# A transformer layer on one core: the first tile gets its own program, and step 0 of the loop moves up in its queues

## The reference

```python
q, k, v = split(x @ w_qkv.T);  q, k = rope(q), rope(k)
scores = (q @ k.T) * 32 ** -0.5;  keep where 0 <= row - key < 64
x = layernorm(x + (softmax(scores) @ v) @ w_out.T)
gate = silu((x @ w_gate) * s_gate);  up = (x @ w_up) * s_up
x = layernorm(x + ((gate * up) @ w_down) * s_down)
```

## Time and profile before

| | us |
|---|---|
| median of 3 runs (lowest, highest) | 1300.38 (1298.34, 1301.97) |
| the profiled execution: its own time | 1294.35 |
| its span, first to last instruction | 1292.5 |
| PE, DVE, ACT, POOL busy | 1212.9, 970.7, 571.3, 377.1 |

### The profile page before, as it was taken

One profiled execution on the slowest core, in us unless ns is written; L12 is line 12 of the kernel. 1 busy time (PEld: TensorE's weight loads), 2 busy tenths in 40 slices (PEclk: granted clock), 3 DMA queues, 4 the chain that ended last, 5 costly groups with the idle time before them and its releaser, 6 DMA issues.

```text
span 1292.5 us, 24588 instructions
## 1 busy us (share of the span) xinstructions
PE 1212.9 (94%) x8200; PEld 548.4 (42%) x8200; DVE 970.7 (75%) x2797; ACT 571.3 (44%) x1608; POOL 377.1 (29%) x370
## 2 busy tenths in 40 slices
PE   8624999999999999999999999999999999999997
PEld 3212444444444444444444444444444444444443
DVE  6855799757997489965897669975799658996543
ACT  1464168502774038810586017840388205870230
POOL 1032115410353104521055102441045210551331
PEclk9855999999999999999999999999999999999999
DMA  9953484334654265441943337542655508443000
GB/s 328 231 109 68 98 151 95 78 64 91 123 95 90 51 114 99 99 86 41 160 101 60 78 80 134 98 87 42 117 107 96 95 34 158 100 65 71 33 1 33
DMA packets 345912, 124.74 MB, mean 97 GB/s; under 512 B 309056, under 2 KB 329792, under 8 KB 345792
## 3 DMA queue, kind: packets, MB, share of 16 engines
q1 hardware_dynamic: 337776, 108.32, 43.9%
q10 hardware_dynamic: 4896, 8.52, 1.8%
q0 software_dynamic: 3120, 6.29, 1.6%
HBM read 27.67 MB, written 8.39 MB: 28 GB/s over the span
## 4 chain that ended last, share of the span: by engine, by line
PE 40%; issue 28%; POOL 11%; DVE 9%; DMA 4%; ACT 4%; SPq 3%; POOLq 0%; DVEq 0%; ACTq 0%
PE bank L420 31%; PE bank L523 6%; POOL xT_sb L363 5%; POOL fuse L368 4%; DMA xT_sb<-xT_sb 2%; DVE fuse L705 2%; PE bank L491 2%; ACT probs L630 2%; DVE fuse L721 1%; SPq L282 1%; DMA qkT<-fuse 1%; DVE largest L833 1%; SPq L288 1%; PE bank L471 1%; POOL x L380 1%
## 5 line engine op out<-in xcount | busy, mean ns | idle before, releaser
L420 PE MATMUL bank<-wqkv,xT_sb 128*128 128x512 f32 x760 | 332.8, 598 | 1.1 <-DMA wqkv<-w_qkvT 0.8
L363 POOL TENSOR_TENSOR xT_sb<-probs,xT_sb 128x512 f16<-128x512 f32 x120 | 142.5, 1187 | 487.1 <-ACT xT_sb L588 487.1
L630 ACT ACTIVATE probs<-bank,neg_max,qk_scale 128x128 f32<-128x128 f32 x512 | 227.2, 455 | 71.1 <-DVE neg_max L761 51.1
L420 PE MATMUL bank<-x1T,wg 128*128 128x512 f16 (+1 forms) x1032 | 243.0, 378 | 0.9 <-DVE ffn_tmp L768 0.9
L420 PE MATMUL bank<-x1T,wu 128*128 128x512 f16 x1024 | 241.9, 379 | 0.0
L588 ACT ACTIVATE fuse<-fuse 128x512 f16<-128x512 f32 x128 | 70.0, 617 | 360.0 <-DVE fuse L711 351.9
L523 PE MATMUL bank<-wd,fuse 128*128 128x512 f16 x1024 | 222.3, 379 | 0.0
L420 PEld LDWEIGHTS bank<-wqkv,xT_sb 128*128 128x128 f32 x760 | 144.0, 191 | 181.4 <-issue 179.1
L368 POOL TENSOR_TENSOR fuse<-ffn_tmp,fuse 128x512 f16<-128x512 f32 x128 | 152.9, 1194 | 71.0 <-ACT fuse L588 69.2
L523 PEld LDWEIGHTS bank<-wd,fuse 128*128 128x128 f16 x1024 | 100.2, 98 | 123.1 <-issue 4.0
L420 PEld LDWEIGHTS bank<-x1T,wu 128*128 128x128 f16 x1024 | 100.2, 98 | 120.6
(11 more groups left out here) (95 smaller groups left out, 1018.8 us busy)
## 6 DMA issues: line engine op xcount, KB each, us to landing
xT_sb<-xT SPq DMA_DIRECT2D x36, 256.0 KB, 4.1
v_cross<-v_own SPq DMA_DIRECT2D x64, 128.0 KB, 2.6
qkT<-x SPq DMA_DIRECT2D x8, 1024.0 KB, 5.8
out<-y ACTq DMA_DIRECT2D x32, 256.0 KB, 2.3
wqkv<-w_qkvT SPq DMA_DIRECT2D x2, 1024.0 KB, 7.2
wd<-w_down POOLq DMA_DIRECT2D x1, 2048.0 KB, 10.7
wg<-w_gate POOLq DMA_DIRECT2D x1, 2048.0 KB, 14.3
wu<-w_up POOLq DMA_DIRECT2D x1, 2048.0 KB, 18.8
```

What stands on the lines that cost most here:

```text
L363: done(probs_low, pool.tensor_tensor(place[:, 1, :, :], probs[:, s % 2, :, :], place[:, 0, :, :], ALU.subtract))
L420: last = pe.matmul(dst, lhsT, rhs, start=(i == 0), stop=(i == len(pairs) - 1))
L630: last = act.activation(probs[:, s % 2, h, :], src, ACT.Exp, bias=neg_max[:, s % 2, h:h + 1], scale=qk_scale[:, 2:3], accum_out=row_sum[:, ...
```

## The change

Body(0) is replaced by a function of its own, `first`, on each engine; the body then serves the loop and the end alone.

In `first`, PE projects blocks 0 and 1 (even, odd, v of each), starts the scores of steps 0 and 1, and projects block 2 and block 3 between the steps; `project_o` of blocks 0, 1 and 2 stands behind steps 8, 12 and 15. The projections go round four banks (0 to 3). Rope of blocks 2 and 3 stands on DVE behind steps 1 and 5, `split_high` likewise on ACT. The low halves of blocks 1 to 3 are made by POOL, in the four subtractions that DVE made before; block 0 stays with DVE. The exponentials have four buffers instead of two; the two fp16 halves have two places instead of four; the transposed ones have four instead of two. The maximum of the next tile's x is found before the steps and spread together with that of the v weights, so that its load is issued ahead of s_down and w_out. SP loads the next tile's x behind step 7. ACT runs one small copy at the start.

In the loop, the weights of step 0 move ahead of the `split_v` of block 3 on DVE; `keep_probs_high` of step 0 moves from behind the exponentials of step 1 to behind the tanh of step 0; `turn_probs` of steps 0 and 1 move ahead of `cross_v` of blocks 2 and 3. PE does `project_o` of blocks 0 and 1 together ahead of the last two `weigh_v`, and `keep_o` of the last pair stands one block later. The rows of x come in four DMAs behind steps 6 to 9 instead of one behind step 6.

The diff, cut to its core:

```diff
+        def qk_banks(j, ffn):
+
+            first = 2 * (j % 2) if ffn else 3 * j % QKV_BANKS
+            return bank32[first], bank32[(first + 1) % QKV_BANKS]
+
...
+        def split_place(s, ffn):
+
+            return xT_slots[s % 2] if ffn else y_slots[s % 2]
+
+        def probsT_place(s, ffn):
+
+            return xT_slots[2 + s % 2] if ffn else x1_slots[s % NB]
+
+        def wait_probsT(eng, a, s, ffn):
+
+            if ffn:
+                wait(probsT_in[s % 2], eng, a - 1, 16 * (s // 2 + 1) - 1)
+            else:
+                eng.wait_ge(first_probsT_in[s % NB], 16 * (s // NB + 1))
...
+        def probs_place(s, ffn):
+
+            if ffn or s % 4 < 2:
+                return probs[:, s % 2, :, :]
+            return ffn_tmp[:, s % 2, :].rearrange("p (h c) -> p h c", h=HG)
...
+            def load_rows(a, j):
+                if j == 0:
+                    wait(scores_done, sp, a, 2 * NG - 1)
+                sp.dma_start(x_rows[:, j, :], x[bass.ds(a * TILE + j * P, P), :]).then_inc(rows_in, 16)
...
             def turn_probs(a, s, ffn):
-                wait(pv_done, sp, a, s - 2)
+                wait(pv_done, sp, a, s - 2 if ffn else s - NB)
                 sp.sem_inc(passed, 1)
                 wait(probs_low, sp, a, s)
                 sp.sem_inc(passed, 1)
-                sp.dma_start_transpose(probsT[s % 2].rearrange("p z h c -> p (z h) c"),
+                sp.dma_start_transpose(probsT_place(s, ffn).rearrange("p z h c -> p (z h) c"),
                                        split_place(s, ffn).rearrange("p z h c -> p (z h c)"))\
-                    .then_inc(probsT_in[s % 2][0], 16)
+                    .then_inc(probsT_in[s % 2][0] if ffn else first_probsT_in[s % NB], 16)
 
...
+            sp.dma_start(next_xT.rearrange("p (k s) -> p k s", k=KC),
+                         xT.rearrange("(k p) s -> p k s", p=P)[:, :, TILE:2 * TILE]).then_inc(next_xT_in, 16)
             sp.dma_start(sdown[:, :], s_down.to_broadcast([P, EMB])).then_inc(sdown_in, 16)
             sp.dma_start(wout[:, :, :], w_outT.rearrange("(k p) n -> p k n", p=P)).then_inc(wout_in, 16)
+
+            def first():
+                a = 0
+                turn_qk(a, 0)
+                turn_qk(a, 1)
+                cross_v(a, 0)
+                cross_v(a, 1)
+                for s in range(STEPS):
+                    turn_probs(a, s, False)
+                    if s == 1:
+                        turn_qk(a, 2)
+                    if s == 3:
+                        cross_v(a, 2)
+                    if s == 5:
+                        turn_qk(a, 3)
+                    if s == 7:
+                        cross_v(a, 3)
+                        for j in range(NB):
+                            load_xT(a + 1, j, False)
+                    if s >= STEPS - NB:
+                        load_rows(a, s - (STEPS - NB))
 
             def body(t, attn, ffn):
                 a, f = t, t - 1
...
                 if attn:
                     for j in range(NB):
                         turn_qk(a, j)
-                        if j:
+                        if 1 <= j < NB - 1:
                             cross_v(a, j - 1)
-                    cross_v(a, NB - 1)
                     for s in range(STEPS):
                         turn_probs(a, s, ffn)
-                        if s == 2 * NG - 2:
-                            wait(scores_done, sp, a, 2 * NG - 1)
-                            sp.dma_start(x_rows, tile_rows(a)).then_inc(rows_in, 16)
+                        if s < 2:
+                            cross_v(a, NB - 2 + s)
+                        if 0 <= s - (2 * NG - 2) < NB:
+                            load_rows(a, s - (2 * NG - 2))
...
+            def split_low(a, j):
+                for i in range(4):
+                    wait(qk_high, pool, a, 4 * j + i)
+                    last = pool.tensor_tensor(*low_operands(j, i), ALU.subtract)
+                done(qk_low, last)
+
...
+            def first():
+                a = 0
+                split_low(a, 1)
+                for s in range(STEPS):
+                    split_probs(a, s, False)
+                    if s == 1:
+                        split_low(a, 2)
+                    if s == 5:
+                        split_low(a, 3)
+                for j in range(NB):
+                    invert_deviation1(a, j)
+                for j in range(NB):
+                    keep_x1(a, j)
...
+            def project_even(a, j, ffn):
 
                 wait_xT(pe, a, j)
+                if ffn:
+                    wait(*((proj_read, pe, a - 1, 2 * j + 1) if j < 2 else (rope_read, pe, a, j - 2)))
+                elif j >= 2:
+                    wait(v_low, pe, a, j - 2)
+                even, _ = qk_banks(j, ffn)
+                for k in range(KC):
+                    if j == 0 and not ffn:
                         pe.wait_ge(wq_even_in[k], 16)
+                    pe.matmul(even, xT_sb[:, j, k, :], wqkv[:, k, 0:EMB], start=(k == 0), stop=(k == KC - 1))
+
+            def project_odd(a, j, ffn):
+
+                if not ffn:
+                    if j == 0:
+                        pe.wait_ge(wq_odd_in, 16)
+                    wait(rope_read, pe, a, j - 1)
+                done(qk_done, qkv(j, 1, qk_banks(j, ffn)[1]))
 
             def project_v(a, j, ffn):
 
-                if j == 0:
+                if not ffn:
+                    if j == 0:
+                        pe.wait_ge(wv_in, 16)
+                    wait(rope_read, pe, a, j - 1)
+                elif j == 0:
                     wait(exp_done, pe, a - 1, STEPS - 1)
-                    if not ffn:
-                        pe.wait_ge(wv_in, 16)
-                done(v_done, qkv(j, 2, bank32[V_BANKS[j]]))
-
-            def scores(a, s):
+                done(v_done, qkv(j, 2, v_bank(j, ffn)))
...
+            def first():
+                a, ffn = 0, False
+                for j in range(2):
+                    project_even(a, j, ffn)
+                    project_odd(a, j, ffn)
+                    project_v(a, j, ffn)
+                scores(a, 0, ffn)
+                scores(a, 1, ffn)
+                project_even(a, 2, ffn)
+                project_odd(a, 2, ffn)
+                for s in range(STEPS):
+                    if s + 2 < STEPS:
+                        scores(a, s + 2, ffn)
+                    if s >= 2:
+                        weigh_v(a, s - 2, ffn)
+                    if s == 0:
+                        project_v(a, 2, ffn)
+                    if s == 2:
+                        project_even(a, 3, ffn)
+                    if s == 3:
+                        project_odd(a, 3, ffn)
+                    if s == 4:
+                        project_v(a, 3, ffn)
+                    if s in (8, 12, 15):
+                        project_o(a, (s - 7) // NG if s < 15 else 2, ffn)
+                weigh_v(a, STEPS - 2, ffn)
+                weigh_v(a, STEPS - 1, ffn)
+                project_o(a, NB - 1, ffn)
+
             def body(t, attn, ffn):
                 a, f = t, t - 1
 
                 if attn:
-                    project_qk(a, 0, ffn)
-                    project_qk(a, 1, ffn)
-                    project_v(a, 0, ffn)
-                    project_qk(a, 2, ffn)
-                    project_v(a, 1, ffn)
-                    project_qk(a, 3, ffn)
-                    project_v(a, 2, ffn)
-                    scores(a, 0)
-                    scores(a, 1)
-                    project_v(a, 3, ffn)
+                    for j in range(NB):
+                        project_even(a, j, ffn)
+                        project_odd(a, j, ffn)
+                        if j:
+                            project_v(a, j - 1, ffn)
+                    scores(a, 0, ffn)
+                    scores(a, 1, ffn)
+                    project_v(a, NB - 1, ffn)
...
+                    project_o(a, 0, ffn)
+                    project_o(a, 1, ffn)
+                    weigh_v(a, STEPS - 2, ffn)
+                    weigh_v(a, STEPS - 1, ffn)
+                    project_o(a, 2, ffn)
+                    project_o(a, 3, ffn)
...
+            def exponentials(a, s, ffn):
                 wait(bias_done, act, a, s)
-                wait(probs_low, act, a, s - 2)
+                wait(probs_low, act, a, s - 2 if ffn else s - 4)
...
+                if s >= 2:
+                    wait_probsT(act, a, s - 2, ffn)
...
+            def first():
+                a, ffn = 0, False
+                split_high(a, 0)
+                split_high(a, 1)
+                keep_v(a, 0, ffn)
+                keep_v(a, 1, ffn)
+                for s in range(STEPS):
+                    exponentials(a, s, ffn)
+                    if s:
+                        keep_probs_high(a, s - 1, ffn)
+                    if s in (1, 5):
+                        split_high(a, 2 + s // NG)
+                    if s in (2, 6):
+                        keep_v(a, 2 + s // NG, ffn)
+                keep_probs_high(a, STEPS - 1, ffn)
```

(60 more changed lines are left out.)

359 lines of the change are left out of this document (152 added, 207 removed).

## The result

The changed kernel takes **1307.81 us** (median of 5 runs, 1306.47 to 1311.22) against 1298.34 for the kernel before (5 runs, 1296.82 to 1301.97). The ratio is 1.007, 95% interval 1.0048 to 1.0092. I had said 1295.0, and the time lies outside my range of 1286 to 1304. The profiled execution took 1308.68, with a span of 1306.9.

The account below looks back on a forecast made before the run. PE, busy 94% of the span, bounds the kernel, except in the first tile, where a chain sets the pace. Profiled 1294.35 + 7 (first tile) - 12 (loop) = 1289.4, plus 6.0 to the median: 1295.4 us, range 1286 to 1304.

Parts of the forecast that it names:

- The first tile: Before the loop: the next tile starts at 143.8 instead of 136.8, +7 us, bounds -1 to +13.
- The walk: First tile: followed step by step from 46.1 us through each engine's order to the next tile's start at 143.8.
- the four products behind gaps: First tile: block 3's v and `project_o` of 0, 1 and 3 take 5.7 us; at full clock 3.7, giving 8 back.
- the first rival: First tile no longer than before, PE busy enough for full clock: -1 instead of +7, 1287 us; chance 0.25.
- The 8.4 us go: Loop: PE's waits for the transpose at `weigh_v` of step 0, 8.4 us over seven bodies, disappear.
- Which rhythm a body falls into hangs on hundredths ...; I keep three or four of seven: Loop, step 2: three or four of seven bodies stay slow, `weights` behind POOL's subtraction; 5.6 us kept.
- a rival: Loop: step 0's waits go but all seven bodies are slow, -6 + 7, 1301 us; chance 0.2.
- A slow body keeps 1.6: Loop: a slow body's loss after the change, 1.05 + 3.0 - 1.4 - 1.0 = 1.6 us.
- head start: Loop: DVE is ahead by 1.4 us, from its ended step 0 wait and held step 1 weights, less 0.2.
- The slower rival: Loop: the slow rhythm takes the head start too, 4.1 us per body, +11 + 7, 1318 us; chance 0.12.
- the 12 that I had named as a sign of being wrong: Loop: the forecast is wrong if PE waits more than 12 us there.
- 6.0 from the profiled execution to the median: Whole kernel: the median stands 6.0 us above the profiled execution, added to 1289.4 for 1295.4.

Follow-up runs that it names:

- e2: Kernel before with only the loop's moves, first tile and row DMAs as they were: 1296.6 us, ratio 0.9975.
- e7: Kernel before with the loop's moves and a wait that starts POOL's subtraction behind `weights`, first tile as before: 1274.6 us, ratio 0.9834.
- e1: Changed kernel with the loop's order put back, new first tile and four row DMAs kept: 1319.4 us, ratio 1.0152.
- e4: Kernel before with 52 tiny memsets at the start of DVE's program, nothing else: 1302.6 us, ratio 1.003.
- e6: Changed kernel with 48 memsets at DVE's start and a wait that starts POOL's subtraction behind `weights`: 1279.5 us, ratio 0.9868.
- e8: Kernel before with only a wait that starts POOL's subtraction behind `weights` in the loop: 1289.2 us, ratio 0.9919.

## Why the prediction was wrong

**The first tile** I had at +7, in bounds of -1 to +13; it measured +4.9. The walk held, each milestone 1.6 to 2.6 us early: exponentials of step 2 at 63.1 (I said 64.9), `weigh_v` of step 2 at 79.8 (81.4), POOL's last subtraction of block 3 at 93.4 (95.1), `weigh_v` of step 6 at 100.4 (103), next tile at 141.7 (143.8). The first milestone already has 1.8 of these, and the four products behind gaps took 5.0 to 6.7 us, 5.7 on average as I had assumed. One sign failed: I had the clock at 0.50 in most windows from 50 to 135. In windows of 10 us it is 0.50 to 0.66 in three (60, 90 and 110) and 0.82 to 1.00 in the other five from 50 to 130. That PE is kept busy enough, as the first rival says, is true for a part of the tile, and it gave nothing back where the sum had its four products. Granted clock of the changed kernel, for the earlier trace rows:

```profile
PEclk9777899999999999999999999999999999999999
```

The timeline of POOL in the changed kernel has the four subtractions of block 2 between two halves of the steps, 4.95 for the four as in the sum, and the same for block 3.

```profile
65.49 1.35 POOL L419 TENSOR_TENSOR y<-probs,y 128x512 f16<-128x512 f32 x1 [12.95 <-ACT y L691]
66.81 4.95 POOL L441 TENSOR_TENSOR fuse<-fuse 128x512 f16<-128x512 f32 x4
71.72 2.25 POOL L419 TENSOR_TENSOR y<-ffn_tmp,y 128x512 f16<-128x512 f32 x2
...
88.47 4.94 POOL L441 TENSOR_TENSOR fuse<-fuse 128x512 f16<-128x512 f32 x4
```

**"The 8.4 us go"**: right, no wait at step 0 remains.

**"Which rhythm a body falls into hangs on hundredths ...; I keep three or four of seven"**: this step failed. With the moves all seven bodies are slow, in e2, where nothing else is changed, as in the changed kernel. The timeline of body 2 of the changed kernel shows the state, POOL 0.18 ahead:

```profile
349.53 1.15 POOL L424 TENSOR_TENSOR fuse<-ffn_tmp,fuse 128x512 f16<-128x512 f32 x1
```

```profile
349.71 1.52 DVE L855 SCALAR_TENSOR_TENSOR probs<-probs,inv_sum 128x512 f32<-128x512 f32 x1
```

I had written the reason under a rival, that nothing holds ACT back at step 2 any more, and gave it 0.2. It fits (in e7, where PE paces, ACT's tanh waits 0.63 for PE; in the changed kernel's body 2 the tanh at 356.93 waits for nothing), but no run delayed ACT alone, and e1 and e4 are slow throughout without the moves, so that part is argued and not shown.

**"A slow body keeps 1.6"**: wrong size. I priced it as 1.05 and 3.0 less a head start of 1.4 and 1.0 of cover. Bodies 1 to 6 of e2 take 152.8 on average, those of e7 149.3: a slow body keeps 3.5. So all slow gives e2 a gain of 2 by the medians and not the 6 of the rival. Its profiled execution even has 4.1 more than that of the kernel before from the start of tile 2 on (1159.9 against 1155.8), because that one, at 1294.35, was 4 below the median.

**What I had no term for**: the jump back, and without it the changed kernel takes about what the kernel before does (1299.4 with memsets). The new first tile has twelve DVE operations fewer ahead of the loop, as many as the subtractions that it gives to POOL; the loop begins at 304 instead of 316, each jump back waits for two pieces of the program instead of one, and that costs 8.4 us in the changed kernel. The same idle costs the kernel before 14.4. It stood in the profile as 16.4 us of "issue" behind L864, and no sum of mine asked what it depends on.

The sum as the runs have it: first tile +4.9 (e6 against e7), moves with the rhythm all slow -1.8 (e2), long idle +8.4: +11.5, against 9.5 measured; the two that are over are less than the uncertainty of one of these medians' ratios. The terms do not simply add, either: with the long idle already there the moves are worth 11.6 and not 2 (e1 at 1319.4, the changed kernel at 1307.8), because the idle costs the old order 14.4.

**The slower rival** (1318, chance 0.12) came nearest in the loop: it had 4.1 per body, and (1165.2 - 1136.7) / 7 = 4.1 is what the changed kernel loses against e7's loop. The waits of PE in the seven bodies are 23.1 us, near twice the 12 that I had named as a sign of being wrong; by body they are 2.5 to 4.1, so that its condition, over 3 in each, holds in four. But its cause was not the whole: the head start was lost at the jump back, before the first step. Its total is 10 too high mostly because I counted 6.0 from the profiled execution to the median on top, where the changed kernel has -0.9. Those 6 us were no constant: the kernel before ran from 1290.5 to 1306.6 in 22 runs, and with the wait alone (e8) from 1285.5 to 1291.1 in 10. So a part of its scatter went with the wait; that its short executions are those with fewer slow bodies was not traced.

The Trainium skill, SBUF — State Buffer, section Who interferes with whom, has the first to start hold the other for the whole operation. The trace agrees: `weights` takes 1.52 us behind POOL's 1.15 started 0.18 ahead, and 0.69 when POOL is made to wait. Each of the 42 in the changed kernel that took over 1.2 us has a subtraction of POOL started ahead of it and still running; e7 and e8 have none that long.

## What to carry to other kernels

Where two engines exclude each other and either can be first, try fixing the order by a wait before you move anything else: here one wait on an engine with time to spare made earlier starts worth some 14 us that were worth 2 in the kernel before without it. Compare idle time by "issue" at the head of a loop on each engine that has no slack, in both kernels, and count the packets of the instruction queue in it; where it moved, a few empty instructions ahead of the loop tell in one run whether the edit or its place is being measured. And before you take one profiled execution for the kernel, look where it lies among the runs: here it was 4 to 6 us below the median before and 1 above it after.

## What the runs showed of the hardware that I had not expected

- DVE's idle at the loop's jump back has two sizes, 2.6 to 2.8 and 4.8 to 5.2 us, by the number of instructions ahead of the loop: long at 304 and 432, short at seven places from 310 to 368. One packet of 8 KB of the instruction queue starts in the short one and two in the long one, at all 108 jumps traced. Memsets in a wait of the prologue moved the time by -7.5 and +14.4 us.
- Two engines that alternate can hold one of two rhythms for a whole body of 16 steps. In the kernel before the body takes 150.7 to 151.9 us in the one and 153.5 to 153.8 in the other; with the moves 149.3 (e7) and 152.8 (e2).
- A wait added to POOL, which the profile of the kernel before shows busy 29% of the time, narrowed that kernel's runs from a spread of 16.1 us (22 runs) to 5.6 (10 runs, e8). The other kernels with it spread 1.0 to 5.7 in 4 to 7 runs; the changed kernel without it spread 4.8 in 5, so not every kernel here had that scatter.
